# Mixture of layer 3 rebuilt around a slot map and adding scatters; self-attention in one straight run

## The chip, the cores and the metric

The kernel runs on one core of a Trainium2 chip. The metric is the device time of one launch in microseconds (us), the median over runs. In every run the whole program is executed: four layers, each of an attention and a feed-forward part.

## The reference, cut to what matters

The input `x` is 2 x 1024 tokens of 256 features in float32: 2048 tokens, 16 tiles of 128. Each layer adds `tanh(gate) * attention(layernorm(x))` and then `tanh(gate) * ffn(layernorm(x))` to `x`. The change touches layer 3 alone. Its attention part is a block of causal self-attention and cross-attention to 64 context rows, each with a small feed-forward part behind it:

```python
q = jnp.einsum('bsc,hcd->bhsd', xn, wq); k, v likewise        # 16 heads of 32
a = jax.nn.softmax(jnp.einsum('bhsd,bhtd->bhst', q, k) * D ** (-0.5), axis=-1)
if causal: a = a * mask                                        # the mask comes after the softmax
```

Since the mask comes behind the softmax, each row's maximum and sum are over all 1024 keys, and only the part below the diagonal is multiplied with the values. The feed-forward part of layer 3 is a mixture with the two best of eight experts for each token, plus a shared expert:

```python
probs = jax.nn.softmax(xn @ router_w, axis=-1)
topv, topi = jax.lax.top_k(probs, 2); topv = topv / jnp.sum(topv, axis=-1, keepdims=True)
for e in range(8): out = out + comb[:, e:e + 1] * swiglu(xn, gate_up_w[e], down_w[e])
out = out + swiglu(xn, shared_gate_up_w, shared_down_w)        # gate clipped to +-10, silu(gate) * up
```

An expert is 256 -> 2 x 1024 -> 256, the shared one 256 -> 2 x 256 -> 256.

## The kernel before, in words

The stages run one after the other; each is a block in which SP, POOL (gpsimd), PE (tensor), ACT (scalar) and DVE (vector) have instruction streams of their own, tied by semaphores. A stage's order is written out by hand. `ps` is PSUM with 8 banks, called `banks` in the profile.

**Cross-attention** (`stage_attention`, L336) folds the key weights into the queries (`fold_q`). Where `narrow` is false (L353; true for head width 16, so in layer 2) it folds the output weights into the values as well (`fold_v`, stored at L570): then 8 matmuls of 256 columns give a tile's output directly. Where it is true, values and output weights stay apart: 8 matmuls of 64 columns wide give the heads of a tile in a bank of their own, ACT stores them (`heads`, L708), 4 matmuls with the output weights follow, and the normalisation's transposes of the next tile (L222) wait in PE's order behind it. Layer 3 has head width 32, layer 0 has 64.

**Self-projection** (`stage_self_project`, L2028) computes queries, keys (in three bfloat16 parts each) and values, and writes them to DRAM by entry, an entry being 4 heads of one batch: `ENTRIES` = 8. SP issues eight DMAs for each pair of tiles k and, for batch 0 (k below 4), eight more into a ninth entry (`places`, L2064), so that the loop of the next stage can load one entry past the end. ACT's stores of the values (L2139) wait for the transfers out of their staging buffer. `load_entry` (L2015) loads an entry with 17 DMAs.

**Self-attention** (`stage_self_attention`, L2196) goes over 8 entries x 32 units (4 heads x 8 tiles of 128 queries). A unit v is: PE `scores` (L2292, 4 matmuls of 512 columns into two banks), DVE maximum (L2390), ACT exponential with row sum (L2373), DVE reciprocal (L2397), POOL multiplication by it (L2273) and mask (L2276), PE `turn` (L2308, 1 to 8 transposes of 128x128, up to four to a bankful), storing of them by ACT (L2359) or DVE (L2361), and `output` (L2326, four heads' matmuls for each chunk of 128 keys). The scores have two places, banks 0-1 and 2-3: `scores(v)` waits until the exponential of v-2 has read its place. Banks 4 and 5 take the turned tiles, banks 6 and 7 the outputs. PE's order for each v is scores(v), turn(v-5), a quarter of an output. ACT stores the outputs. Four entries make a body, and a hardware loop (`Fori`) runs it twice; at its turn the pipeline drains.

**The mixture** (`stage_experts`, L727, called for layer 3 as `l3f`) works in this order. PE computes router logits. DVE chooses the two best experts and, from counts by PE (`counted`, L961), works out for each token and choice a row number, a slot (DVE, L1159 to L1271). POOL scatters all rows of `xn` to those slots in DRAM by 32 indirect DMAs (L922) while PE runs the shared expert (L973, L984; eight pairs of tiles). Then come 24 expert tiles: 15 of 256 rows and 9 of 128 rows, 39 blocks of 128 rows in all (4992 rows for 4096 used). For each, SP loads the rows and the expert's weights, PE transposes (L999), computes hidden units (L1012, 64 matmuls) and output (L1025, 32 or 16), with DVE's clip (L1302), ACT's silu (L1077) and DVE's product between; ACT stores the result and POOL sends it to DRAM (L930). At the end POOL gathers 32 times (L939) the result rows of each token, DVE multiplies them by the routing weight and adds them to x (L1322), and SP sends x out by tile.

## Time and profile before

| what | value |
|---|---|
| median of 3 runs | 2548.7 us (2547.37 to 2549.26) |
| the profiled execution, its own time | 2524.31 us |
| span of its profile | 2522.6 us |
| mean granted TensorE clock | 0.902 |
| busy, share of the span | PE 81%, DVE 54%, ACT 37%, POOL 28% |
| DMA packets, data | 171504, 219.20 MB |
| chain that ended last | PE 17%, POOL 2%, issue 1%, DVE 1%, DMA 1% |

Time of the profiled execution is 2524.31 us, 1.7 us beyond its span. It lies 24.4 us (1.0%) under the median of the timed runs. The chain is the page's own: it starts in layer 3's mixture, so it says nothing of the stages before. A busy PE is one with matmuls in flight; the granted clock says at what speed, 0.9 being the mean in tenths of full speed.

### The profile page before, as it was taken

The numbers are of one execution on the slowest core, as the hardware profiler recorded it, in microseconds if no ns is written. First come the engines' busy times: TensorE is split into PE (matmuls) and PEld (weight loads), VectorE is DVE, ScalarE is ACT, GpSimd is POOL, SyncE is SP. The second block draws the span as 40 slices with busy tenths as digits, with TensorE's granted clock in tenths as the row PEclk, the third lists the DMA queues.
The fourth block names the chain that finished last, engine by engine and source line by source line (L and its number), as shares of the span: only waits on it lengthen the run. The fifth ranks groups of instructions, "written<-read, shape, count | busy, mean of one in ns | idle before, by whom it ended". The sixth has DMA issues, their size and how long they took to land. (4 is left out here: it accounts for less than half of the span.)

```text
span 2522.6 us, 36317 instructions
## 1 busy us (share of the span) xinstructions
PE 2047.2 (81%) x11904; PEld 1504.7 (60%) x11904; DVE 1367.6 (54%) x3511; ACT 929.6 (37%) x1859; POOL 710.5 (28%) x1199
## 2 busy tenths in 40 slices
PE   5983974467867677999799979969898589999991
PEld 4661863354444454555455558846687378888991
DVE  4871006535745765888688847757636432222332
ACT  4220321112324346888688843232232112222230
POOL 0223011030130125777577751102330230000005
PEclk9995995578979789999999989979999699999995
DMA  2004531000011286333333430110000525555684
GB/s 87 1 1 150 167 104 28 13 13 14 1 19 12 82 216 165 85 85 85 86 65 92 97 108 11 28 36 1 1 13 1 193 104 175 175 175 175 215 287 115
DMA packets 171504, 219.20 MB, mean 87 GB/s; under 512 B 39911, under 2 KB 133540, under 8 KB 165184
## 3 DMA queue, kind: packets, MB, share of 16 engines
q1 hardware_dynamic: 163344, 196.65, 26.7%
q0 software_dynamic: 7264, 20.31, 2.5%
q8 instruction: 88, 1.44, 0.2%
q14 instruction: 88, 0.72, 0.1%
q10 hardware_dynamic: 720, 0.07, 0.0%
HBM read 171.13 MB, written 46.14 MB: 86 GB/s over the span
## 5 line engine op out<-in xcount | busy, mean ns | idle before, releaser
L2390 DVE TENSOR_REDUCE l3s_mx<-banks 128x1 f32<-128x1024 f32 x256 | 313.1, 1223 | 96.7 <-PE banks L2292 93.8
L2292 PE MATMUL banks<-l_stack 128*128 128x512 bf16 x1024 | 268.1, 385 | 44.1 <-ACT xn_tokens L2373 21.0
L1012 PE MATMUL banks<-l3f_xrt,l3f_w 128*128 128x256 f32 (+1 forms) x1536 | 277.9, 342 | 2.7 <-issue 1.5
L1012 PEld LDWEIGHTS banks<-l3f_xrt,l3f_w 128*128 128x128 f32 x1536 | 249.6, 192 | 29.1 <-issue 3.3
L1302 DVE TENSOR_SCALAR l3f_sg<-banks 128x256 f32<-128x256 f32 (+1 forms) x192 | 72.0, 375 | 287.5 <-PE banks L1012 287.5
L2273 POOL TENSOR_TENSOR xn_tokens<-xn_tokens,l3s_sm 128x1024 f32<-128x1024 f32 (+3 forms) x128 | 201.6, 1575 | 50.3 <-DVE l3s_sm L2397 49.2
L222 PE MATMUL banks<-ident,xn_tokens 128*128 128x128 f32 x320 | 64.7, 338 | 166.8 <-DVE xn_tokens L211 148.0
L2292 PEld LDWEIGHTS banks<-l_stack 128*128 128x128 bf16 x1024 | 80.8, 98 | 163.3 <-ACT xn_tokens L2373 52.6
L2373 ACT ACTIVATE xn_tokens<-banks,l3s_mx 128x1024 f32<-128x1024 f32 x128 | 142.7, 1115 | 46.2 <-DVE l3s_mx L2390 45.1
L222 PEld LDWEIGHTS banks<-ident,xn_tokens 128*128 128x128 f32 x320 | 46.6, 172 | 188.4 <-DVE xn_tokens L211 133.0
L2373 ACT ACTIVATE x_features<-banks,l3s_mx 128x1024 f32<-128x1024 f32 x128 | 143.0, 1117 | 27.9 <-DVE l3s_mx L2390 27.6
L1077 ACT ACTIVATE l3f_sg<-l3f_sg 128x256 f32<-128x256 f32 (+1 forms) x192 | 72.2, 376 | 208.9 <-DVE l3f_sg L1302 208.9
L1025 PE MATMUL banks<-l3f_w,l3f_ht 128*128 128x256 f32 x624 | 138.5, 379 | 0.0
L930 POOL DMA_DIRECT2D l3f_results<-l3f_yt x24 | 15.8, 658 | 410.7 <-ACT l3f_yt L708 410.7
L1025 PEld LDWEIGHTS banks<-l3f_w,l3f_ht 128*128 128x128 f32 x624 | 116.8, 190 | 14.9
L2537 PE MATMUL banks<-x_features,weights 128*128 128x256 f32 x512 | 117.5, 390 | 4.3 <-ACT x_features L235 2.4
L2308 PEld LDWEIGHTS banks<-ident,xn_tokens 128*128 128x128 f32 x832 | 96.5, 140 | 29.1 <-issue 10.2
L2550 PE MATMUL banks<-weights,l3m_ht 128*128 128x256 f32 x512 | 113.2, 379 | 0.4 <-DVE l_x L2605 0.4
L2308 PE MATMUL banks<-ident,xn_tokens 128*128 128x128 f32 x832 | 112.6, 273 | 0.5 <-ACT l3s_pt L2359 0.5
L2537 PEld LDWEIGHTS banks<-x_features,weights 128*128 128x128 f32 x512 | 100.1, 196 | 19.5 <-issue 3.8
L2273 POOL TENSOR_TENSOR x_features<-x_features,l3s_sm 128x128 f32<-128x128 f32 (+3 forms) x128 | 92.4, 722 | 65.6 <-DVE l3s_sm L2397 64.6
L2359 ACT ACTIVATE l3s_pt<-banks 128x384 f32<-128x384 f32 (+2 forms) x192 | 97.0, 505 | 24.2 <-PE banks L2326 18.5
(532 smaller groups left out, 3925.4 us busy)
## 6 DMA issues: line engine op xcount, KB each, us to landing
l3f_w<-in_L_ffn_gate_up_w_dram SPq DMA_DIRECT2D x24, 2048.0 KB, 7.6
l3f_w<-in_L_ffn_down_w_dram SPq DMA_DIRECT2D x24, 1024.0 KB, 6.0
l_stack<-l_q_part SPq DMA_DIRECT2D x72, 256.0 KB, 6.0
l_stack<-l_k_part SPq DMA_DIRECT2D x72, 256.0 KB, 11.4
l0f_w<-in_L_ffn_W_dram SPq DMA_DIRECT2D x16, 1024.0 KB, 5.8
l_q_part<-l_stack SPq DMA_DIRECT2D x24, 256.0 KB, 3.0
l_k_part<-l_stack SPq DMA_DIRECT2D x24, 256.0 KB, 3.7
l3f_rows<-l3f_zero SPq DMA_DIRECT2D x13, 384.0 KB, 4.1
```

Source lines behind the costliest of these rows:

```text
L222: last = nc.tensor.transpose(ps[:, bank, c * PAIR + u * P:c * PAIR + (u + 1) * P], src(2 * j + u)[:, c * P:(c + 1) * P], core["ident"][:, :])
L1012: last = nc.tensor.matmul(ps[:, f % 4, h * PAIR:h * PAIR + size], w1_sb[:, p, dc, h * FF + f * P:h * FF + (f + 1) * P], xrt[:, p, dc, 0:si ...
L1025: last = nc.tensor.matmul(ps[:, 4 + p, u * D:(u + 1) * D], ht[:, p, f, u * P:(u + 1) * P], w2_sb[:, p, f, :], start=(f == 0), stop=(f == F ...
L1077: nc.scalar.activation(sg[:, f % 4, 0:size], sg[:, f % 4, 0:size], ACT.Silu).then_inc(silued, 1)
L2273: nc.gpsimd.tensor_tensor(ex[v % RING][:, si * P:], ex[v % RING][:, si * P:], sm[:, v % RING:v % RING + 1].to_broadcast([P, TOK - si * P]) ...
L2292: last = nc.tensor.matmul(ps[:, 2 * (v % 2) + h, :], stack[p][0][s][:, r, si * P:(si + 1) * P], stack[p][1][s][:, r, h * 512:(h + 1) * 512 ...
L2308: last = nc.tensor.transpose(ps[:, 4 + n % 2, c * P:(c + 1) * P], ex[v % RING][:, (si + c0 + c) * P:(si + c0 + c + 1) * P], core["ident"][ ...
L2359: last = op.activation(dst, src, ACT.Copy)
L2373: nc.scalar.activation(ex[v % RING][:, :], ps[:, 2 * (v % 2):2 * (v % 2) + 2, :].rearrange("p a n -> p (a n)"), ACT.Exp, bias=mx[:, v % RI ...
L2390: nc.vector.tensor_reduce(mx[:, v % RING:v % RING + 1], ps[:, 2 * (v % 2):2 * (v % 2) + 2, :].rearrange("p a n -> p (a n)"), AX_X, ALU.max ...
L2537: last = nc.tensor.matmul(ps[:, n % 4, 0:PAIR], w2[:, dc, f * P:(f + 1) * P], core["xt"][:, dc, PAIR * j:PAIR * (j + 1)], start=(dc == 0), ...
L2550: last = nc.tensor.matmul(ps[:, 4 + k % ring, u * D:(u + 1) * D], ht[:, k % 2, f, u * P:(u + 1) * P], w3[:, f, :], start=(f == 0), stop=(f ...
```

## The change

`stage_attention` takes the narrow form where the head width is at most 32 (before: at most 16). The self-projection writes no ninth entry. The self-attention is one straight run of 256 units with three places for scores (banks 0 to 5); turned tiles and outputs share banks 6 and 7 in alternation, an output's matmuls are done together, and the outputs are stored by ACT or DVE according to the bank; DVE stores ahead of its maximum. POOL multiplies in the form with a scalar operand.

A new function, `stage_top2`, takes the place of `stage_experts` in layer 3. It writes `xn` to DRAM by token and scatters no rows. From the slots DVE makes two tables, which of the 39 blocks a slot lies in (`spot`) and which of its 128 rows (`low_hot`); 32 matmuls turn them into a map from slot to token (`place`) and to routing weight (`share`). POOL gathers each block's rows by that map from the written `xn`, and after the expert adds them, already scaled by ACT (`store_y`), to the output in DRAM by an indirect DMA with an addition, each after the one before it has landed. The output holds x with the shared expert, written by SP before. The shared expert runs beside the routing: its clip, product and addition are POOL's, its PSUM copies, silu and scaling ACT's. The routing arithmetic up to the slots is the same. All 24 tiles are written out without a loop. Cut to what matters:

```diff
-    narrow = width * 4 <= KEYS
+    narrow = width * 2 <= KEYS
...
+def stage_top2(core, a, plan):
...
+                for h in range(2):
+                    at = slice(h * TILES // 2, (h + 1) * TILES // 2)
+                    sp.dma_start(xn_rows.rearrange("(t p) d -> p t d", p=P)[:, at, :], core["xn"][:, at, :]).then_inc(xn_sent, 16)
...
+                for q in range(PAIRS):
+                    sp.wait_ge(s_added, q + 1)
+                    sp.dma_start(a["out"].rearrange("b (t p) d -> p (b t) d", p=P)[:, 2 * q:2 * q + 2, :],
+                                 core["x"][:, 2 * q:2 * q + 2, :]).then_inc(begun, 16)
...
+                def shared_clip(n):
+                    pool.wait_ge(s_copied, n + 1)
+                    nc.gpsimd.tensor_scalar(su[:, n % 4, 0:PAIR], su[:, n % 4, 0:PAIR], 10.0, -10.0, ALU.min,
+                                            ALU.max).then_inc(s_clipped, 1)
+                def shared_multiply(n):
+                    q = n // SC
+                    pool.wait_ge(s_silued, n + 1)
+                    if q >= 2:
+                        pool.wait_ge(s_out_ready, q - 1)
+                    nc.gpsimd.tensor_tensor(s_ht[:, q % 2, n % SC, :], su[:, n % 4, 0:PAIR], su[:, n % 4, PAIR:2 * PAIR],
+                                            ALU.mult).then_inc(s_hid_stored, 1)
+                def shared_add(q):
+                    pool.wait_ge(s_out_stored, q + 1)
+                    x2 = pair_of(core["x"], q)
+                    nc.gpsimd.tensor_tensor(x2, x2, so[:, q % 2, :], ALU.add).then_inc(s_added, 1)
+                for n in range(SC * PAIRS + 1):
+                    if n < SC * PAIRS:
+                        shared_clip(n)
+                    if n >= 1:
+                        shared_multiply(n - 1)
+                    if n >= 2 * SC and n % SC == 0:
+                        shared_add(n // SC - 2)
+                shared_add(PAIRS - 1)
+                def gather(t):
+                    if t >= 2:
+                        pool.wait_ge(rows_turned, t - 1)
+                    for u in range(units(t)):
+                        at = blocks_through[t] + u
+                        pool.indirect_dma_start(xr[:, t % 2, u, :], None, xn_rows,
+                                                bass.IndirectOffsetOnAxis(ap=place[:, at:at + 1], axis=0),
+                                                bounds_check=T - 1, oob_is_err=False).then_inc(rows_in[t % 2], 16)
+                def scatter_add(t):
+                    pool.wait_ge(y_stored, t + 1)
+                    for u in range(units(t)):
+                        at = blocks_through[t] + u
+                        if at >= 1:
+                            pool.wait_ge(added, 16 * at)
+                        pool.indirect_dma_start(out_rows, bass.IndirectOffsetOnAxis(ap=place[:, at:at + 1], axis=0),
+                                                yt[:, t % 2, u, :], None, bounds_check=T - 1, oob_is_err=False,
+                                                compute_op=ALU.add).then_inc(added, 16)
+                pool.wait_ge(xn_sent, 32)
+                pool.wait_ge(places_made, 1)
+                gather(0)
+                gather(1)
+                pool.wait_ge(begun, 16 * PAIRS)
+                for t in range(tiles):
+                    if t + 2 < tiles:
+                        gather(t + 2)
+                    scatter_add(t)
+                pool.wait_ge(added, 16 * BLOCKS)
...
+                for j in range(PAIRS + 2):
+                    if j < PAIRS:
+                        for f in range(SC):
+                            shared_hidden(SC * j + f)
+                    if j == 2:
+                        pe.wait_ge(made, 9)
+                        pe.wait_ge(chosen, 1)
+                        nc.tensor.matmul(ps[:, 5, 0:P], tri[:, :], hots[:, :, :].rearrange("p t e -> p (t e)"),
+                                         start=True, stop=True)
+                        nc.tensor.matmul(ps[:, 6, 0:P], ones[:, :], hots[:, :, :].rearrange("p t e -> p (t e)"),
+                                         start=True, stop=True).then_inc(counted, 1)
+                    if j >= 2:
+                        shared_output(j - 2)
+                pe.wait_ge(spread, 1)
+                for n in range(2 * TILES):
+                    last = nc.tensor.matmul(ps[:, 7, 0:2 * BLOCKS], low_hot[:, n, :],
+                                            spot[:, n // TILES, n % TILES].rearrange("p a b -> p (a b)"),
+                                            start=(n == 0), stop=(n == 2 * TILES - 1))
+                last.then_inc(mapped, 1)
...
+                def shared_copy(n):
+                    act.wait_ge(s_hid_ready, n + 1)
+                    if n >= 4:
+                        act.wait_ge(s_hid_stored, n - 3)
+                    copy_bank(nc, su[:, n % 4, :], ps[:, n % 2, :]).then_inc(s_copied, 1)
+                def shared_silu(n):
+                    act.wait_ge(s_clipped, n + 1)
+                    nc.scalar.activation(su[:, n % 4, 0:PAIR], su[:, n % 4, 0:PAIR], ACT.Silu).then_inc(s_silued, 1)
+                def shared_store(q):
+                    act.wait_ge(s_out_ready, q + 1)
+                    if q >= 2:
+                        act.wait_ge(s_added, q - 1)
+                    nc.scalar.activation(so[:, q % 2, :], ps[:, 2 + q % 2, :], ACT.Copy, scale=gate).then_inc(s_out_stored, 1)
...
+                def store_y(t):
+                    p = t % 2
+                    act.wait_ge(out_ready, t + 1)
+                    if t >= 2:
+                        act.wait_ge(added, 16 * blocks_through[t - 1])
+                    for u in range(units(t)):
+                        at = blocks_through[t] + u
+                        last = nc.scalar.activation(yt[:, p, u, :], ps[:, 4 + p, u * D:(u + 1) * D], ACT.Copy, scale=share[:, at:at + 1])
+                    last.then_inc(y_stored, 1)
...
+                nc.vector.tensor_copy(flat(slot_i), flat(slot))
+                dve.drain()
+                ts(flat(slot_i), flat(slot_i), 7, None, ALU.arith_shift_right)
+                dve.drain()
+                nc.vector.tensor_copy(flat(slot_hi), flat(slot_i))
+                dve.drain()
+                stt(flat(slot), flat(slot_hi), float(-P), flat(slot), ALU.mult, ALU.add)
+                for k in range(2):
+                    tt(spot[:, k, :, 1, :], iota_hi[:, :].unsqueeze(1).to_broadcast([P, TILES, BLOCKS]),
+                       slot_hi[:, k, :].unsqueeze(2).to_broadcast([P, TILES, BLOCKS]), ALU.is_equal)
+                dve.drain()
+                for k in range(2):
+                    tt(spot[:, k, :, 0, :], spot[:, k, :, 1, :], token[:, :].unsqueeze(2).to_broadcast([P, TILES, BLOCKS]), ALU.mult)
+                dve.drain()
+                for k in range(2):
+                    tt(spot[:, k, :, 1, :], spot[:, k, :, 1, :], weight[:, k, :].unsqueeze(2).to_broadcast([P, TILES, BLOCKS]), ALU.mult)
+                dve.wait_ge(xn_sent, 32)
+                tt(low_hot, iota_lo[:, :].unsqueeze(1).to_broadcast([P, 2 * TILES, P]),
+                   flat(slot).unsqueeze(2).to_broadcast([P, 2 * TILES, P]), ALU.is_equal).then_inc(spread, 1)
+                dve.wait_ge(mapped, 1)
+                ts(place[:, :], ps[:, 7, 0:BLOCKS], float(NONE), None, ALU.add)
+                nc.vector.tensor_copy(share[:, :], ps[:, 7, BLOCKS:2 * BLOCKS]).then_inc(places_made, 1)
...
-                    if b == 0:
-                        places.append((ENTRIES, 1))
...
-    BODY = 4
...
+    SCORES = 3
...
-        with nc.Fori(0, ENTRIES // BODY) as jj:
...
+                    nc.gpsimd.tensor_scalar(ex[v % RING][:, si * P:], ex[v % RING][:, si * P:],
+                                            sm[:, v % RING:v % RING + 1], None, ALU.mult)
...
+                def output(w):
+                    e, si = w // KC, ORDER[w % KC]
+                    n = uses["out", w]
+                    for side in range(2):
+                        pe.wait_ge(stored[side], stored_through(side, max(last_turn[w], n - 2 if side == n % 2 else 0)))
+                    for c in range(si, KC):
+                        for r in range(R):
+                            last = nc.tensor.matmul(ps[r * W:(r + 1) * W, 6 + n % 2, 0:P],
+                                                    values[:, e % 2, c, r * W:(r + 1) * W],
+                                                    pt[:, w % 2, r, c - si, :], start=(c == si),
+                                                    stop=(c == KC - 1))
+                    last.then_inc(out_ready, 1)
...
+                for v in range(ENTRIES * UNITS + OUT):
+                    if v < ENTRIES * UNITS and v % UNITS == 0:
+                        e = v // UNITS
+                        pe.wait_ge(loaded[e % 2], 16 * LOADS * (e // 2 + 1))
+                    if v < ENTRIES * UNITS:
+                        scores(v)
+                    if v >= OUT and (v - OUT) % R == 0:
+                        output((v - OUT) // R)
+                    if TURN <= v < ENTRIES * UNITS + TURN:
+                        turn(v - TURN)
...
+            def _(dve):
+                for v in range(ENTRIES * UNITS + OUT + 1):
+                    store_output(dve, nc.vector, v - 1, 1)
+                    if v >= TURN + 1:
+                        store_turned(dve, nc.vector, v - TURN - 1, 1)
+                    if v < ENTRIES * UNITS:
+                        dve.wait_ge(scores_ready, v + 1)
+                        nc.vector.tensor_reduce(mx[:, v % RING:v % RING + 1],
+                                                ps[:, 2 * (v % SCORES):2 * (v % SCORES) + 2, :].rearrange("p a n -> p (a n)"),
+                                                AX_X, ALU.max, negate=True).then_inc(measured, 1)
+                    if 1 <= v <= ENTRIES * UNITS:
+                        dve.wait_ge(exped, v)
+                        nc.vector.reciprocal(sm[:, (v - 1) % RING:(v - 1) % RING + 1],
+                                             sm[:, (v - 1) % RING:(v - 1) % RING + 1]).then_inc(inverted, 1)
...
-    stage_experts(core, a, "l3f", top=2, full=TOP2_FULL, half=TOP2_HALF, capacity=None, plan=plans["l3f"], following=None,
-                  w1="L3_ffn_gate_up_w", w2="L3_ffn_down_w", swiglu=True, gate=core["gate_ffn"][:, 3:4],
-                  norm_behind=False)
+    stage_top2(core, a, plans["l3f"])
```

## Rows read from the trace of the kernel before

**Rows 1.** The chain that ended last, in order of time: start us, us, what

```profile
2050.68 16.38 PE banks L1012 x64
...
2462.37 6.92 PE banks L1025 x32
```

**Rows 2.** Timeline in self-attention: start us, us, engine, line, operation, out<-in, count [idle before]

```profile
1053.20 0.93 PE L2308 MATMUL banks<-ident,xn_tokens 128*128 128x128 f32 x7
...
1054.06 0.64 PE L2326 MATMUL banks<-l3s_pt,l_values_in 128*32 128x128 f32 x16
...
1054.64 1.04 PE L2292 MATMUL banks<-l_stack 128*128 128x512 bf16 x4
...
1055.57 0.95 PE L2308 MATMUL banks<-ident,xn_tokens 128*128 128x128 f32 x7
...
1056.46 0.42 PE L2326 MATMUL banks<-l3s_pt,l_values_in 128*32 128x128 f32 x8
...
1056.82 1.04 PE L2292 MATMUL banks<-l_stack 128*128 128x512 bf16 x4
...
1062.94 0.38 PE L2308 MATMUL banks<-ident,x_features 128*128 128x128 f32 x2
1063.14 1.22 DVE L2390 TENSOR_REDUCE l3s_mx<-banks 128x1 f32<-128x1024 f32 x1 [0.36 <-PE banks L2292]
...
1063.25 0.64 PE L2326 MATMUL banks<-l3s_pt,l_values_in 128*32 128x128 f32 x16
...
1065.77 0.61 PE L2292 MATMUL banks<-l_stack 128*128 128x512 bf16 x2
```

**Rows 3.** Groups at L2390 (ns min/median/max, first and last start), and the timeline mid-way

```profile
L2390 DVE TENSOR_REDUCE l3s_mx<-banks x256: 1201/1225/1227, 968.9 to 1468.6; 128x1 f32<-128x1024 f32 x128
...
1208.61 1.04 PE L2292 MATMUL banks<-l_stack 128*128 128x512 bf16 x4
...
1225.90 3.59 PE L2292 MATMUL banks<-l_stack 128*128 128x512 bf16 x8 [8.15 <-issue]
```

**Rows 4.** Waits from 825 to 970 us: engine, line <- releaser: us, times, longest

```profile
ACT l_stack L2139 <- DMA l_values<-l3p_vs: 10.5, 2, 9.0
```

**Rows 5.** Timeline of SP's queue: part of one loading of an entry

```profile
1050.60 3.88 SPq L2023 DMA_DIRECT2D l_stack<-l_k_part  x8
```

**Rows 6.** The cross-attentions: one group by form (L570), and timeline rows of PE

```profile
L570 ACT ACTIVATE l3a_fold_v<-banks x16: 384/384/385, 1669.7 to 1683.2; 128x256 f32<-128x256 f32 x16
...
1730.25 3.60 PE L499 MATMUL banks<-l3a_fold_q,x_features 128*128 128x512 f32 x8
1738.02 1.45 PE L499 MATMUL banks<-l3a_fold_q,x_features 128*128 128x512 f32 x3
...
650.22 1.11 PE L222 MATMUL banks<-ident,xn_tokens 128*128 128x128 f32 x4 [3.51 <-ACT l2a_heads L708]
```

**Rows 7.** Timeline of DVE in the routing of the mixture

```profile
1984.03 0.29 DVE L1159 COPY l3f_total<-banks 128x128 f32<-128x128 f32 x1 [0.50 <-PE banks L961]
...
2002.12 0.17 DVE L1271 COPY l3f_slot_f<-l3f_slot_f 128x16 f32<-128x16 f32 x1
```

**Rows 8.** Timeline of PE in the shared expert: two pairs of tiles

```profile
2031.56 3.62 PE L973 MATMUL banks<-x_features,weights 128*128 128x256 f32 x16
...
2036.74 0.59 PE L973 MATMUL banks<-x_features,weights 128*128 128x256 f32 x2
```

**Rows 9.** Timeline in the second feed-forward of layer 3: DVE beside POOL

```profile
1603.58 0.73 POOL L2507 TENSOR_TENSOR l_xo<-l_xo,weights 128x256 f32<-128x256 f32 x1
...
1603.71 0.61 DVE L150 SCALAR_TENSOR_TENSOR l3m_norm_rs<-l3m_norm_t,l3m_norm_rs 128x2 f32<-128x2 f32 x1
```

**Rows 10.** DMA issues of the page: engine, operation, count, KB each, us to landing

```profile
l3f_results<-l3f_yt POOLq DMA_DIRECT2D x15, 256.0 KB, 6.0
...
l3f_rows<-xn_tokens,l3f_slot POOLq DMA_INDIRECT x32, 2.5
```

**Rows 11.** The gathers of the end, grouped: ns min/median/max, first and last start

```profile
L939 POOL DMA_INDIRECT l3f_yg<-l3f_results,l3f_slot x32: 995/1002/1092, 2472.9 to 2513.4; - x32
```

More of the change, by code:

```diff
@@ L2089, in sent_before @@
             def sent_before(k):
-                return sum(16 * 8 * (2 if q < PAIRS // B else 1) for q in range(k % 2, k, 2))
+                return sum(16 * 8 for q in range(k % 2, k, 2))
             @block.gpsimd
@@ L2204, in stage_self_attention @@
     R, W = GROUP, L3_WIDTH
-    BODY = 4
     RING = 8
     TURN = 5
-    STORE = TURN
     OUT = TURN + R + 1
@@ new lines, in store_turned @@
+            def store_turned(eng, op, v, side):
+                if v >= ENTRIES * UNITS:
+                    return
+                e, w = v // UNITS, v // R
+                for g, (u, c0, size) in enumerate(groups):
+                    if u != v % UNITS or uses["turn", e, g] % 2 != side:
+                        continue
+                    n = BANKFULS * e + g
+                    eng.wait_ge(turned, n + 1)
+                    if w >= 2:
+                        eng.wait_ge(out_ready, w - 1)
+                    dst = pt[:, w % 2, v % R, c0:c0 + size, :].rearrange("p c n -> p (c n)")
+                    src = ps[:, 6 + side, 0:size * P]
+                    if side == 0:
+                        last = op.activation(dst, src, ACT.Copy)
+                    else:
+                        last = op.tensor_copy(dst, src)
+                    last.then_inc(stored[side], 1)
@@ new lines, in store_output @@
+            def store_output(eng, op, v, side):
+                if not OUT <= v < ENTRIES * UNITS + OUT or (v - OUT) % R != 0:
+                    return
+                w = (v - OUT) // R
+                e, si = w // KC, ORDER[w % KC]
+                if uses["out", w] % 2 != side:
+                    return
+                eng.wait_ge(out_ready, w + 1)
+                if e >= 2:
+                    eng.wait_ge(out_sent[e % 2], 16 * (e // 2))
+                dst, src = heads_out[:, e % 2, si * P:(si + 1) * P], ps[:, 6 + side, 0:P]
+                last = op.activation(dst, src, ACT.Copy) if side == 0 else op.tensor_copy(dst, src)
+                last.then_inc(stored[side], 1)
@@ L2404, in self_out_weights @@
+        clear_semaphores()
 def self_out_weights(a):
```

588 lines of the change are left out of this document (445 added, 143 removed).

## The prediction

> **What bounds the kernel now.** The page gives PE 81% busy, but its chain begins in the last mixture; so I read the chain for that stage and timelines for the others. In the mixture's main part the chain is PE without a gap [rows 1]: from 2050.68 us to 2462.37 + 6.92 = 2469.29 it takes 418.6 us for 39 blocks, 10.73 us each. What stands ahead (routing) and behind it (gathers) is latency, with PE short of work. In self-attention PE, DVE and ACT share a ring [rows 2, 3]; its 256 maxima span 499.7 us. Two things lie open there: the rate of a unit, and the turn of the loop. In the rest, the rows that the change touches are a wait for stored values [rows 4] and a cross-attention tile [rows 6].
>
> The profiled execution took 2524.3 us, 24.4 (1.0%) less than the median of 2548.7. I work out a difference against the former and subtract it from the latter. A measurement of this kernel can tell about 0.2%, 5 us.
>
> **Self-attention, rate.** By starts on PE [rows 2], seven transposes take 0.86 us (1053.20 to 1054.06), two 0.31: about 0.10 + 0.108 each. Two chunks of output (16 records) take 0.58, one 0.36: 0.14 for a piece and 0.22 for a chunk. Scores take 0.93. An entry has 32 units, 144 transposes, 36 chunks in 26 pieces: 29.8 + 18.8 + 11.6 = 60.1 us, 1.88 a unit. The ring of two score places is nearly as long: from a maximum (1063.14) to the scores that reuse the place (1065.77) 2.63, and 1.04 until they are done, with the hand-over 3.7 to 3.74 for two units, 1.87. Taking for each group of four units the larger of PE and 7.48 gives 60.9 us, 1.903 a unit. The maxima confirm it: 499.7 less the loop's turn (17.1, below) is 482.6 over 254 steps, 1.90.
> After the change an output is one piece: 8 pieces instead of 26 take 2.6 us off, 57.4 an entry, 1.79. Three places stretch the ring to 3.7/3 = 1.25, no bound. New is that turned tiles and outputs share two banks: an output's bank is stored by DVE or ACT before PE may go on with the second bankful. No row shows this; I add 0.04 a unit (a fifth of a 0.2 us wait), bounds 0 and 0.11, the latter eating all the gain. So 1.83, and (1.903 - 1.83) x 255 = 18.6 us.
> **The loop's turn.** Scores at 1208.61 are followed by the next at 1225.90 [rows 3]: 17.3 less one unit of 1.9 is 15.4, and the group behind it runs slower (eight records 3.59 where four take 1.04 [rows 2, 3]), 1.7 more. All 17 go. Together -35.6; bounds -46 (1.79 and 17) and -5 (a rate that gets 0.05 worse).
>
> **Self-projection.** ACT waits 10.5 us in two waits [rows 4] for values to be sent, the longest behind SP's loading of the first entry. SP spends 3.88 us on eight issues [rows 5], 0.49 each; the eight ninth-entry writes of pair 3 stand ahead, 3.9 us of queue and 0.5 MB. -4, bounds 0 (the transfers end last whatever SP does) and -8.
>
> **Cross-attention of layer 3, narrow.** Sixteen stores less, of 0.384 us plus hand-over, 0.43 [rows 6]: -6.9. The values must be built twice over instead: two products of 512 columns and two DVE copies, +2.7. A tile took 7.77 us (1730.25 to 1738.02); a pair of tiles now 16.0. The new one has fewer columns, 14.5, but PE waits behind the stored heads as layer 2's does (3.51 us for ACT) [rows 6], of which a half is filled by the next scores: 16.2. With a longer tail (1.5) +2 net; bounds -6 and +12 (the wait in full at several tiles, then slower scores behind it).
>
> **Mixture, head.** Now: DVE has the counts at 1984.03 and the slots at 2002.12 [rows 7], 82 small instructions in 18.1 us, then POOL scatters and hidden starts at 2050.68 [rows 1]. After: the hidden groups of three pairs stand ahead of the counts, 3 x 3.62 [rows 8] = 10.9, half of it beside DVE's choice of experts: counts at 1989.6. From there DVE runs beside POOL, which has per pair two clips (up to 0.73 each), two products of 0.73 and an addition of up to 1.46 [rows 9]: about 3.7 us of each 5.18 [rows 8]. One row shows what that does: a DVE instruction with two inputs took 0.61 where small ones take 0.17, started 0.13 behind POOL's 0.73 [rows 7, 9]. Of the 82, 49 are of such a kind (two inputs or a scalar operand). So DVE completes about 10.9 of them a pair, and the slots come at 2025, not 2007.6. Behind them: split and tables, 6 operations of 624 elements and one of 4096, 10.6 -> 2035.6; the map's 32 products, as 32 of 128 columns 6.9 (16 of 256 columns take 6.92 [rows 1]), at half that speed 13.8, I take 9.5 -> 2045; places 0.6; two gathers, 1.3 and 2.5 [rows 10, 11] -> 2050; transposes and their store 2.0 -> 2052.1. The 32 scatters of 1.3 and the load behind them are gone, yet the head ends 1.5 us later. SP's two writes of xn and its eight of x (issue 0.49 each) lie beside this; if cover fails, the eight delay only POOL's first addition into the output, not PE.
> The Trainium skill (SBUF — State Buffer, Who interferes with whom) has the shared port pair as an exclusive lock, and counts DVE's copies and casts among what takes it, which no row here shows; by that 75 of the 82 are blocked and the head gives +5.5 instead of +1.5. It has a chance of its own below.
>
> **Mixture, main part.** The same tiles and PE work: 0. What covers the new parts: POOL has per full tile two gathers (1.3 each) and two additions into DRAM, each issued when the last has landed; a plain store lands in 6.0 beside the weights, a lone scatter in 2.5 [rows 10]. At 1.3 + 2.5 to 1.3 + 6.0 a block takes 3.8 to 7.3, with its gather 5.1 to 8.6, under 10.73.
> The Trainium skill (Collectives: The Full Stack, The bandwidth ceiling: the fold count and why AG ≠ RS ≠ AR) says that an addition in the DMA path needs two source reads and gets about half the throughput. No row here shows it; doubling the landing would lead to the slower rival below.
>
> **Mixture, tail.** Now from 2469.3 to the span's end 2522.6, 53.3 us, most of it 32 gathers at 1.31 (2472.9 to 2513.4) [rows 11]. After: store 0.6, the previous addition's rest 2, issue 1.0, landing 3 (bounds 2.5 and 12), closing 2.8: 9. -44.3, bounds -47 and -30.
>
> **Sum.** -35.6 - 4 + 2 + 1.5 + 0 - 44.3 = -80.4: the profiled execution at 2443.9, the median at 2468.3.
>
> **Rivals.**
> A. *The lock does not bite*: the row of 0.61 is chance, or POOL's new work finds gaps. The slots come at 2007.6; then the shared expert, PE-bound, ends about 2026 and the chain gives hidden at 2037.5, -13 instead of +1.5. Sum -95, 2454. For it: most small DVE operations in the trace last 0.17; against: POOL is hardly ever busy beside them now. 0.15.
> B. *Copies and casts are locked out too*: +5.5, sum -76, 2472. 0.07.
> C. *Shared banks take the place of the score ring*: PE waits for each output's store, the unit stays at 1.903; only the loop's turn is gained. -80.4 + 18.6 = -62, 2487. For it: DVE stores an output a unit late, and its 1.22 us maximum stands in front [rows 2]. 0.15.
> D. *Slower: the additions become a serial chain.* They are strictly one after the other, 39 of them. If one takes L, 39 L binds once L is above 10.73, and the kernel is slower than before from 39 L = 414.8 + 80, L = 12.7. Rows give 3.8 to 7.3; with a landing of twice 6.0 it is 1.3 + 12 = 13.3, and POOL's gathers queue behind the wait. At L = 14: +131 - 80 = +51, 2600. 0.06.
> E. *Nothing is gained*, because the straight program's instruction stream or an unseen wait gives it all back: within 5 us of 2548.7. 0.02.
>
> **How the numbers follow.** The forecast has 0.55; its own range, from the bounds of the terms (self-attention and tail mostly), is 2448 to 2490. A, B and C lie at 2454, 2472 and 2487, so a range of 2432 to 2500 holds them with their own spread and leaves out D and E and both far ends. Faster by over 0.2%: 0.55 + 0.15 + 0.07 + 0.15 = 0.92; within: 0.02; slower: 0.06.
>
> **What would show it.** In self-attention: maxima spanning about 467 us, no gap mid-way, PE's waits at L2292 for ACT gone; waits for stored bankfuls would show C. In the head: DVE's small operations at 0.3 to 0.6 beside POOL, the map's products near 2036 to 2045 (times relative to the stage's begin), hidden 87 us behind that begin; at 72 it is A. In the main part 10.7 a block; idle PE behind late gathers would show D, read from the additions' issue to landing. The tail about 9 us. I am wrong if the main part grows, or if self-attention stays near 1.90 a unit.

## The result, and the profile after

The changed kernel takes 2557.3 us (median of 7 runs, 2550.6 to 2561.3) against 2546.3 for the kernel before, in the same runs: ratio 1.0043, 95% interval 1.0028 to 1.0058. It is slower by 0.4%, where the forecast was faster by 3.2%; the measured time lies 57 us above the upper end of the range, 2500. The profiled execution took 2550.6 us with a span of 2549.1.

I cut both profiles at the same marks: begin of the self-projection (tiles `l3p`), first maximum and last maximum of self-attention (DVE's group of L2390, now L2953), SP's first load of the next stage (tiles `l3m`), begin of the cross-attention (tiles `l3a`), first store of router logits, DVE's first copy of the counts, first hidden product and last output product of the mixture. Differences of those starts, in us:

| stretch | before | after | forecast of the difference | measured |
|---|---|---|---|---|
| begin to self-projection | 818.5 | 815.6 | 0 | -2.9 |
| self-projection to first maximum | 150.5 | 147.8 | -4 | -2.7 |
| first to last maximum | 499.7 | 540.0 | -35.6 | +40.3 |
| last maximum to the next stage | 12.8 | 18.0 | 0 | +5.2 |
| self-attention's feed-forward | 179.4 | 178.2 | 0 | -1.2 |
| cross-attention and its feed-forward | 308.4 | 301.7 | +2 | -6.7 |
| logits to hidden (routing) | 81.4 | 82.2 | +1.5 | +0.8 |
| first hidden to last output product | 418.6 | 453.9 | 0 | +35.3 |
| to the span's end | 53.4 | 11.6 | -44.3 | -41.8 |

Two rows carry the miss: self-attention (with the 5.2 us behind its last maximum) and the mixture's main part. The costliest groups of the page of after; behind the bar: busy us, mean ns | idle before, releaser:

```profile
L2953 DVE TENSOR_REDUCE l3s_mx<-banks 128x1 f32<-128x1024 f32 x256 | 311.2, 1218 | 75.8 <-PE banks L2852 75.0
L2837 POOL TENSOR_SCALAR xn_tokens<-xn_tokens,l3s_sm 128x1024 f32<-128x1024 f32 (+3 forms) x128 | 303.0, 2367 | 15.2 <-DVE l3s_sm L2958 15.2
...
L2837 POOL TENSOR_SCALAR x_features<-x_features,l3s_sm 128x128 f32<-128x128 f32 (+3 forms) x128 | 139.1, 1086 | 0.1
```

POOL's two groups are busy 442 us of self-attention's 540, and with the 256 masks of 0.29, 75 us, it has next to no idle time: it waited 15 us for the first unit and then for nobody.

In the mixture's main part I read the distance from one tile's transposes to the next. Where [rows 1] had PE without a gap, the chain of after goes through DMAs. At the change from full tiles (256 rows) to half tiles (128 rows):

```profile
2405.31 5.40 DMA out_dram<-l3f_yt,l3f_place
...
2413.35 6.75 DMA l3f_xr<-l3f_xn,l3f_place
...
2420.83 8.81 PE banks L1614 x32
```

POOL still issues the two additions of a full tile, the second when the first has landed, and a gather behind them, while PE has only a half tile's hidden units (7.31 us instead of 13.98) to fill the time. PE idled 9.3 us there, and 9.3 once more a tile later. A little later, one half tile around, the timeline shows the round trip with one addition (start us, us, engine, line):

```profile
2463.64 0.47 ACT L1686 ACTIVATE l3f_yt<-banks,l3f_share 128x256 f32<-128x256 f32 x1 [2.34 <-PE banks L1614]
...
2464.89 1.58 POOL L1509 DMA_INDIRECT out_dram<-l3f_yt,l3f_place  x1 [7.85 <-ACT l3f_yt L1686]
...
2466.78 1.07 POOL L1499 DMA_INDIRECT l3f_xr<-l3f_xn,l3f_place  x1 [0.31 <-issue]
...
2471.98 0.44 PE L1588 MATMUL banks<-ident,l3f_xr 128*128 128x128 f32 x2 [1.23 <-DMA l3f_xr<-l3f_xn,l3f_place]
...
2475.91 0.47 ACT L1686 ACTIVATE l3f_yt<-banks,l3f_share 128x256 f32<-128x256 f32 x1 [2.65 <-PE banks L1614]
```

A result is stored, POOL issues its addition (1.58), then the gather of the rows that PE transposes next (in the program it is three tiles on from the one just stored); the rows land 5.2 us later, PE transposes them, and only behind those transposes stands the next output. From store to store: 12.27 us, where the kernel without this wait (e3 below) takes 10.82.

### The profile page after: what moved, and what is told of

It reads as the page before. It is cut to its first block and busy times, and to the rows that moved or that the text cites. A ratio compares the mean times of both kernels' runs of the same rounds, so it can differ in the third digit from the quotient of the medians.

```text
span 2549.1 us, 35782 instructions
## 1 busy us (share of the span) xinstructions
PE 2031.5 (80%) x12060; PEld 1506.6 (59%) x12060; DVE 1362.3 (53%) x3476; ACT 946.5 (37%) x1865; POOL 909.5 (36%) x1235
## 5 line engine op out<-in xcount | busy, mean ns | idle before, releaser
L2953 DVE TENSOR_REDUCE l3s_mx<-banks 128x1 f32<-128x1024 f32 x256 | 311.2, 1218 | 75.8 <-PE banks L2852 75.0
L2837 POOL TENSOR_SCALAR xn_tokens<-xn_tokens,l3s_sm 128x1024 f32<-128x1024 f32 (+3 forms) x128 | 303.0, 2367 | 15.2 <-DVE l3s_sm L2958 15.2
L222 PE MATMUL banks<-ident,xn_tokens 128*128 128x128 f32 x320 | 64.3, 336 | 173.4 <-DVE xn_tokens L211 147.8
L1509 POOL DMA_INDIRECT out_dram<-l3f_yt,l3f_place x39 | 62.1, 1593 | 347.7 <-ACT l3f_yt L1686 275.5
L2868 PE MATMUL banks<-ident,xn_tokens 128*128 128x128 f32 x832 | 126.1, 282 | 68.7 <-POOL xn_tokens L2840 60.6
L2868 PEld LDWEIGHTS banks<-ident,xn_tokens 128*128 128x128 f32 x832 | 89.3, 140 | 124.9 <-POOL xn_tokens L2840 100.4
L222 PEld LDWEIGHTS banks<-ident,xn_tokens 128*128 128x128 f32 x320 | 45.7, 171 | 196.5 <-DVE xn_tokens L211 126.0
L2912 ACT ACTIVATE l3s_pt<-banks 128x384 f32<-128x384 f32 (+3 forms) x224 | 109.4, 489 | 115.8 <-PE banks L2868 115.2
L2852 PEld LDWEIGHTS banks<-l_stack 128*128 128x128 bf16 x1024 | 101.0, 99 | 82.2 <-issue 16.2
L2837 POOL TENSOR_SCALAR x_features<-x_features,l3s_sm 128x128 f32<-128x128 f32 (+3 forms) x128 | 139.1, 1086 | 0.1
L1614 PEld LDWEIGHTS banks<-l3f_w,l3f_ht 128*128 128x128 f32 x624 | 120.2, 196 | 16.3
L2914 DVE COPY l3s_pt<-banks 128x384 f32<-128x384 f32 (+3 forms) x160 | 88.1, 551 | 56.6 <-PE banks L2868 55.5
```

What stands on the lines that cost most here:

```text
L222: last = nc.tensor.transpose(ps[:, bank, c * PAIR + u * P:c * PAIR + (u + 1) * P], src(2 * j + u)[:, c * P:(c + 1) * P], core["ident"][:, :])
L1614: last = nc.tensor.matmul(ps[:, 4 + p, u * D:(u + 1) * D], ht[:, p, f, u * P:(u + 1) * P], w2_sb[:, p, f, :], start=(f == 0), stop=(f == F ...
L2837: nc.gpsimd.tensor_scalar(ex[v % RING][:, si * P:], ex[v % RING][:, si * P:], sm[:, v % RING:v % RING + 1], None, ALU.mult)
L2852: last = nc.tensor.matmul(ps[:, 2 * (v % SCORES) + h, :], stack[p][0][s][:, r, si * P:(si + 1) * P], stack[p][1][s][:, r, h * 512:(h + 1) ...
L2868: last = nc.tensor.transpose(ps[:, 6 + n % 2, c * P:(c + 1) * P], ex[v % RING][:, (si + c0 + c) * P:(si + c0 + c + 1) * P], core["ident"][ ...
L2912: last = op.activation(dst, src, ACT.Copy)
```

## The experiments

My theory after this reading: two independent losses, POOL's scalar form in self-attention and the gather that stands behind the addition.

### e1_gather_ahead, e2_pool_two_inputs, e3_both

e1:

```diff
                 gather(1)
+                gather(2)
                 pool.wait_ge(begun, 16 * PAIRS)
                 for t in range(tiles):
-                    if t + 2 < tiles:
-                        gather(t + 2)
+                    if t + 3 < tiles:
+                        gather(t + 3)
                     scatter_add(t)
```

e2:

```diff
-nc.gpsimd.tensor_scalar(ex[v % RING][:, si * P:], ex[v % RING][:, si * P:],
-                        sm[:, v % RING:v % RING + 1], None, ALU.mult)
+nc.gpsimd.tensor_tensor(ex[v % RING][:, si * P:], ex[v % RING][:, si * P:],
+                        sm[:, v % RING:v % RING + 1].to_broadcast([P, TOK - si * P]), ALU.mult)
```

e3 has both. Expected:

> The changed kernel, with each tile's gathers issued one step earlier, ahead of the addition that they stood behind. Theory 1 (a loop: output, store, addition, gather of the tile after next, its transposes, which stand ahead of the next output on PE): the loop is cut, full tiles go from 21.5 to 21.2 us, half tiles from 12.2 to 10.8, the main part from 450 to about 420, the kernel from 2557 to about 2527. Rival (the additions themselves are the chain, 39 of them one after the other, or they slow the gathers' transfers): the main part stays at 440 or more, the kernel above 2545.

> The changed kernel, with POOL's multiplication in self-attention in the form of before (two inputs, the second spread along the row) instead of the scalar operand. Theory 1 (POOL bounds self-attention since the scalar form takes 2.37 us where the other took 1.58): the 256 maxima span about 468 us instead of 540, the kernel comes to about 2485. Rival (the shared banks, or the new order, hold PE back, and POOL is only busy): the span stays above 520, the kernel above 2535. If between, both: about 490 us would be the old rate of 1.90.

> Both edits together. Theory 1: the two losses are independent and add up: about 2557 - 30 - 72 = 2455, faster than before by 3.6%; the prediction's sum was 2468. Rivals: each as above; above 2500 if either holds.

Measured: e1 2518.7 us, ratio to the kernel before 0.9893 (0.9874 to 0.9912); e2 2483.2, 0.975 (0.9731 to 0.9769); e3 2450.0, 0.9621 (0.9603 to 0.9639). In e1 the main part is 418.1 us instead of 453.9, in e2 the maxima span 476.9 instead of 540.0; each leaves the other stretch as it was to within 3 us, and together they take 107 us off. Both rivals fall: neither a chain of additions nor the shared banks made the kernel slow. What the earlier issue did is seen in the waits of PE's weight loads (PEld) for the gathers in the main part, first of after, then of e3 (us, times, longest):

```profile
PEld banks L1588 <- DMA l3f_xr<-l3f_xn,l3f_place: 33.2, 19, 9.5
```

```profile
PEld banks L1589 <- DMA l3f_xr<-l3f_xn,l3f_place: 0.2, 1, 0.2
```

### e4_before_scalar_form

The kernel before with e2's edit the other way round. Expected:

> The kernel before, with only POOL's multiplication in the scalar form. Theory 1: POOL needs 2.02 us and gaps, some 2.1 us a unit, above the 1.90 that the score ring gave: the maxima span about 540 + 15 us for the loop's turn, the kernel 2546 + 50 = 2596. Rival (the form costs only in the new order): within 10 us of 2546.

Measured: 2608.5 us, ratio 1.0242 (1.0223 to 1.0261); the maxima span 556.5 us, 56.8 more. The form costs much the same in either order: 57 us of span and 63 of the median here; in the new order 63 us of span and 69 to 74 of the median (e1 against e3, after against e2). Some 5 us of it lie behind the last maximum (there 21.6 us to the next stage's first product where e13, the kernel before again, has 16.3). The groups of POOL by form in e4 and in the kernel before (ns min/median/max, the largest form has 1024 elements):

```profile
L2273 POOL TENSOR_SCALAR xn_tokens<-xn_tokens,l3s_sm x128: 1884/2365/2858, 970.4 to 1524.2; 128x1024 f32<-128x1024 f32 x32, 128x896 f32<-128x896 f32 x32, 128x768 f32<-128x768 f32 x32, 128x640 f32<-128x640 f32 x32
```

```profile
L2273 POOL TENSOR_TENSOR xn_tokens<-xn_tokens,l3s_sm x128: 1254/1576/1897, 971.8 to 1465.0; 128x1024 f32<-128x1024 f32 x32, 128x896 f32<-128x896 f32 x32, 128x768 f32<-128x768 f32 x32, 128x640 f32<-128x640 f32 x32
```

1024 elements take 2.86 us in the form with a scalar from memory and 1.90 with two inputs: (2.858 - 1.884) / 384 = 2.5 ns an element against 1.7.

### e5_two_places

`SCORES = 2` in e3. Expected:

> e3_both with two places for scores instead of three; turned tiles and outputs still share banks 6 and 7. In e3_both the 256 maxima span 477 us, 1.87 a unit, where the prediction had 1.83 and PE's own work 1.79. Theory (the third place earns the gain, the shared banks cost some of it): with two places the ring's 1.87 and the shared banks' waits come together, 1.92 to 2.0 a unit, a span of 490 to 510, the kernel 13 to 33 us above e3_both. Rival (the third place does nothing, all of the gain is the loop's turn): the span stays within 4 us of 477.

Measured: 2500.2 us; the maxima span 526.3, 2.06 a unit, more than expected. So in the new order the third place earns 0.19 a unit, not 0.03 (1.90 before, 1.87 in e3): with two places the new order is slower than the old one. The reason is argued, not shown by a run of its own: DVE's stores now stand ahead of its maximum and ACT's stores of outputs ahead of its exponential, and these stores lengthen the ring of scores. Waits of PE's weight loads from 1000 to 1400 us in e5, then in e3 (us, times, longest):

```profile
PEld banks L2853 <- ACT xn_tokens L2943: 50.5, 72, 1.2
```

```profile
PEld banks L2881 <- ACT l3s_pt L2913: 31.1, 27, 1.6
```

In e5 the scores (L2853) wait for the exponential; in e3 that wait is gone from the list and the output (L2881) waits longer for the stores of turned tiles instead (15.3 us in e5).

### e6_plain_scatter

The addition of e3 left out (`compute_op` gone). Expected:

> e3_both with the indirect DMA of the results into the output as a plain write instead of an addition (what lies there already is overwritten, so the other expert's share and x are left out). Theory (an addition costs the DMA path a second read, but nobody waits for it since the gathers are ahead): POOL's wait for the landing of a tile's first one falls from 4.6 us to 2 to 4, the main part stays at 418, the kernel within 5 us of e3_both. Rival (the addition is no dearer than a write): the wait stays at 4.6.

Measured: 2448.3 us, main part 417.8. POOL's waits for a landing, counted from the end of its issue, are 71.4 us in 15 waits, in e3 68.9 in 15. The rival holds for the landing: beside the weights' loading an addition lands no later than a write. The issue itself is dearer, 1.58 us against 1.02, so from one issue to the next that waits for it 6.2 us pass instead of 5.7 (medians). The Trainium skill's rule that an addition needs two source reads and so gets half the throughput (Collectives: The Full Stack, The bandwidth ceiling: the fold count and why AG ≠ RS ≠ AR; stated there for large collectives) does not show at this size, 128 KB by rows of 1 KB.

### e7_pool_two_columns

```diff
-nc.gpsimd.tensor_scalar(su[:, n % 4, 0:PAIR], su[:, n % 4, 0:PAIR], 10.0, -10.0, ALU.min,
+nc.gpsimd.tensor_scalar(su[:, n % 4, 0:2], su[:, n % 4, 0:2], 10.0, -10.0, ALU.min,
```

and likewise for product and addition, so that most of POOL's work on the shared expert is left out; ACT's silu writes `s_ht`. Expected:

> e3_both with POOL's clip, product and addition of the shared expert on 2 columns only (the product and most of the clip and of the addition are left out; ACT's silu writes what PE reads). Theory (POOL locks DVE out while routing is worked out): from the counts to the slots 18 to 19 us instead of 30, to the first hidden unit 46 to 52 instead of 65, of which part is that the map's products follow PE's work without a gap and so run at the higher clock (7 us instead of 14); the kernel 13 to 19 us below e3_both. Rival (DVE is slow for another cause, such as PE's traffic): 28 us or more to the slots, the kernel within 4 us of e3_both.

Measured: 2435.1 us; 48.4 from counts to hidden instead of 64.9. DVE in after, with a POOL row of the same time:

```profile
2018.62 0.29 DVE L1746 COPY l3f_total<-banks 128x128 f32<-128x128 f32 x1 [2.73 <-PE banks L1570]
...
2021.11 1.27 POOL L1483 TENSOR_TENSOR x_tokens<-x_tokens,l3f_so 128x512 f32<-128x512 f32 x1 [2.77 <-ACT l3f_so L1652]
2021.21 1.20 DVE L1779 COPY l3f_rows_f<-l3f_scan 128x8 f32<-128x8 f32 x1
...
2050.36 1.16 DVE L1848 CAST l3f_slot_hi<-l3f_slot_i 128x32 f32<-128x32 int32 x1
```

A copy of 8 elements takes 1.20 us while POOL adds for 1.27. The same cast in e7, and the map's products in after and in e7:

```profile
1969.66 0.18 DVE L1851 CAST l3f_slot_hi<-l3f_slot_i 128x32 f32<-128x32 int32 x1
...
1984.38 7.27 PE L1578 MATMUL banks<-l3f_spot,xn_tokens 128*128 128x78 f32 x64
```

```profile
2061.74 13.94 PE L1577 MATMUL banks<-l3f_spot,xn_tokens 128*128 128x78 f32 x64 [9.44 <-DVE xn_tokens L1861]
```

The cast takes 0.18 instead of 1.16: DVE was held back by POOL, copies and casts included. And the products take half the time when they follow PE's other work.

### e8_wide_l3a and e12_ninth_entry

Two parts of the change undone in e3: `narrow = width * 4 <= KEYS`, and the writes of the ninth entry. Expected:

> e3_both with layer 3's cross-attention in its form of before. From its begin to the router's logits of the mixture e3_both takes 302.1 us and the kernel before 308.4. Theory (the narrow form itself saves 6 us, where the prediction had a loss of 2): back to 308, the kernel 6 us above e3_both. Rival (the difference comes from another place, such as what the stage before leaves): within 2 us.

> e3_both with the ninth entry's writes restored. From the self-projection's begin to the first maximum: 147.1 us in e3_both, 150.5 in the kernel before. Theory (the writes stand ahead of SP's loading): back to 150.5, the kernel 3 us above e3_both; within the noise of the median, but seen in the profile. Rival (the 3 us come from the loop's setup): 147 stays.

Measured: e8 2459.7 us, 311.2 from the cross-attention's begin to the logits instead of 302.1: the narrow form saves 9, a little more than expected. e12 took 149.5 us from the self-projection's begin to the first maximum instead of 147.1, so the writes cost 2.4. Its median, 2458.5, is 8.5 above e3's, of which this explains a third; stretches that the edit does not touch were longer as well (821.8 instead of 816.2 up to the self-projection). I take the stretch, and leave the rest open.

### e10_filler_twice

```diff
+                for n in range(20):
+                    nc.tensor.matmul(ps[:, 4, 0:PAIR], s1[:, 0, 0:P], core["xt"][:, 0, 0:PAIR], start=True, stop=True)
                 pe.wait_ge(spread, 1)
```

and 12 more ahead of the first tile's transposes. Expected:

> e3_both with matmuls whose result nobody reads, 20 ahead of the map's products and 12 ahead of the first tile's transposes, so that PE is not idle before them. In e3_both PE idles 9.4 us, then the map's 32 products take 13.95 us at a granted clock of 0.50; where they followed work without a gap (POOL on 2 columns) they took 7.27. Theory (the idle time costs the clock): the map takes 7 us, the first tile's hidden products 14 instead of 15.6, from counts to hidden 57 to 58 instead of 64.9, the kernel 7 to 10 us below e3_both. Rival (the products are slow in themselves, through their weights, and the fillers only delay): the same or up to 8 us slower.

Measured: 2441.2 us, ratio 0.9591 (0.9578 to 0.9604), 57.8 us from counts to hidden. The windows of after around the map and of e10 (us, PE, PEld, DVE, ACT and POOL busy, granted clock, DMA share, GB/s):

```profile
2048.00:2062.00 14.00, 2.26 (x9) 1.70 (x10) 12.81 (x13) 1.68 (x3) 4.58 (x6) 0.78 1.02 397
2062.00:2076.00 14.00, 13.68 (x64) 13.46 (x64) 0.28 (x2) 0.00 (x0) 0.00 (x0) 0.50 0.53 181
```

```profile
1995.00:2003.00 8.00, 7.79 (x67) 7.74 (x68) 0.46 (x3) 0.00 (x0) 0.00 (x0) 1.00 0.99 338
```

In after PE was busy 2.3 of 14 us, and the products behind ran at a granted clock of 0.50, the 1.2 GHz level, and took 13.94 us. With matmuls nobody reads in that gap the same products ran at 1.00, 2.4 GHz, and took 7.37 us. The rival falls.

### e11_output_later and e14_all_together

e11 is e3 with `OUT = TURN + R + 2`; e14 has e10's and e11's edits. Expected:

> e3_both with each output of self-attention one unit later (OUT one more). In e3_both PE waits at the output for ACT's and DVE's stores of turned tiles, some 50 us over 400. Theory (the output stands too close behind the last store in the shared banks): the waits halve and the maxima span 465 to 473 us instead of 477. Rival (what is waited for is the store of the use just before in the same bank, which moves along): the same within 3 us, or slower.

> e3_both with both later edits, the matmuls that keep PE busy in the head and the outputs one unit later. Theory (they work in different stages and add up): the maxima span 469 us, 57.8 from counts to hidden, the kernel 2449 - 8 - 7 = 2434. Rival (one's gain is given back, as layer 3's cross-attention took 2.6 us longer in the profile of e11): 2440 or more.

Measured: e11 2442.9 us, the maxima span 468.6, 1.84 a unit. The weight loads' waits at the output for ACT's stores fall from 31.1 to 12.3 us between 1000 and 1400; new ones for POOL's masks appear, 23.7 us. e14: 2434.1 us, ratio 0.9553 (0.9539 to 0.9567), maxima 468.8, counts to hidden 57.7: the gains add up. e14 is the fastest of the complete kernels here, 4.5% below the kernel before.

### e13_before_again and e15_four_scatters

The profile that the prediction used lay 22 us under its kernel's median. e13 is the kernel before, unchanged; e15 leaves 28 of the mixture's 32 scatters out. Expected:

> The kernel before, unchanged, profiled again. Its profile gave 2524.3 us, 22 below its median of 2546; the other kernels' profiles lie 2 to 7 below theirs. The kernel before with the scalar form showed, while POOL issued its 32 scatters, two stretches of 9.0 and 14.3 us in which DVE stood still beside the shared expert, and 91.8 us from counts to hidden instead of 66.6. Theory (DVE stands still behind POOL's scatters in most executions, once or twice, and the profiled one was a lucky one): this profile is near 2541 to 2546, with 80 to 92 us from counts to hidden. Rival (the profile is low in general and the stretch belongs to the scalar form): about 2524 again, 66.6 us.

> The kernel before with 4 of the mixture's 32 scatters of rows (the others are left out; their rows stay zero, and the expert tiles do the same work on them). The kernel before, profiled again, had DVE's clip of the shared expert standing still for 8.4 and 15.0 us while POOL issued the scatters, and 91.9 us from counts to hidden. Theory (POOL's issuing of indirect transfers holds DVE's instruction back): no such wait; PE's shared expert then sets the head, 18 us to the slots, some 42 us of shared expert, 2 behind it: 62 to 66 us from counts to hidden, the kernel 25 to 30 us below the one before, at about 2518. Rival (the stand-still comes with something else, such as the loading of weights or of code at that time): 80 us or more, within 10 us of 2546.

Measured: e13 2548.5 us, its profiled span 2545.5 with 91.9 us from counts to hidden, where the first profile had 66.6. All other stretches agree within 2 us. In e13:

```profile
2031.07 0.42 DVE L1276 TENSOR_SCALAR l3f_sg<-banks 128x256 f32<-128x256 f32 x1 [8.42 <-remote]
...
2046.45 0.42 DVE L1276 TENSOR_SCALAR l3f_sg<-banks 128x256 f32<-128x256 f32 x1 [14.96 <-remote]
...
2047.25 3.23 PE L973 MATMUL banks<-x_features,weights 128*128 128x256 f32 x7 [26.83 <-DVE l3f_ht L1284]
```

DVE stands still twice, 23.4 us together, and PE waits with it. The first stand-still lies within POOL's issues of its scatters, one every 1.28 us (2001.5 to 2042.2); the second begins there and ends 4.2 us behind the last one. e15: 2513.3 us, ratio 0.9867 (0.9848 to 0.9886), 62.5 us from counts to hidden and no such wait: 35 us under the kernel before where 25 to 30 were expected, 29 of them in this stretch against e13. So it comes with the scatters. The first profile caught an execution without it; its 2524.3 us lie below every timed run of the kernel before (2538 to 2553), and the two later profiles of this head (e4, e13) both have it. e15 takes the issues, the transfers and whatever queues behind them away together: which of these holds DVE back (the loading of code, named in the rival, is not excluded), and why it did not in that one execution, no run here shows.

## Why the prediction was wrong

**Self-attention, POOL.** The sum had no term for "POOL multiplication becomes the scalar form", though the diff shows it; it was silently costed at nothing. It makes POOL the bound: 540.0 / 255 = 2.12 us a unit. The cover was thin: before, POOL had 294.0 us of multiplication and 75 of masks in 499.7; with the new form the same work is 442 + 75 = 517 us, more than the stretch had. This is the largest error, 540.0 - 476.9 = 63 us, and the 5.2 behind the last maximum go with it.

**Self-attention, rate and loop's turn.** With the form of before the span is 477, and I had 467 (1.83 against 1.87). The turn of the loop was right: 17 of the 23 us saved are the gap of [rows 3], the rest is the rate. The term that was mis-sized is the shared banks' 0.04: if PE's own 1.79 is right, 0.08 is left for it. Moving the output by a unit gets 0.03 back. Rival C had the right banks and not the right wait: it had PE wait for the store of an output (7.4 us of the weight loads' waits in e3's 400), and PE waits ahead of the output for stores of turned tiles (31.1 for ACT's). "Three places stretch the ring to 1.25" was too favourable, since the ring became longer in the new order: with two places it runs at 2.06, not 1.87.

**Mixture, main part.** The step that failed is "a block takes 3.8 to 7.3, with its gather 5.1 to 8.6, under 10.73". Its numbers were right: an addition takes 1.6 + 4.6 = 6.2 us. But I compared POOL's throughput with PE's, and the order makes a round trip of latencies: output, store, addition, gather, landing (5.2, not the 2.5 of [rows 10]), transposes, next output. 3.47 + 0.47 + 0.8 + 1.9 + 5.2 + 0.4 gives 12.2 for a half tile; measured 12.27 where PE needs 10.82. In a full tile there is a second addition and gather, and it takes 21.4 to 21.6 instead of 21.16. These steady tiles are the smaller part: against e3 the full tiles lose 6 us (2.5 of them in one tile, where a landing was late) and the last half tiles 6. The other 24 of the 36 us are lost in the three tiles at the change of size, where a full tile's two additions and a landing of 6.7 us stand against a half tile's work: two waits of 9.3, and outputs behind them that take 9.00 and 6.22 us instead of 7.07 and 3.62, at granted clocks of 0.75 and 0.58. An average of 10.73 a block hides that place. Rival D saw gathers behind the wait, but priced it by the additions' chain, which alone never bound.

**Mixture, head.** Forecast +1.5, measured +0.8 against the same profile: luck, with errors that cancel. Counts came 2.4 us later, not 5.6; 30.2 us from there to the slots, not 35.4; the tables 12.9, not 10.6; the map 13.95, not 9.5, because PE idled before it. Rival B was right about the kinds: the copy of 1.20 and the cast of 1.16 above agree with the lock of the Trainium skill (SBUF — State Buffer, Who interferes with whom), which counts copies and casts in; e7 shows the whole price of POOL's work beside DVE, 16.5 us, of which 6.7 are the map's clock. Its sum of +5.5 was still further off than +1.5, since the other errors cancel. Rival A falls.

**Mixture, tail.** -41.8 for -44.3: after the last output product 11.6 us remain, not 9 (the terms of the 9 add up to 9.4). The last addition is issued at 2538.85, 1.4 us behind it, and 10.2 us before the span's end, where I had 1 + 3 + 2.8.

**Cross-attention.** -6.7 for +2. The loop was right: 16.46 us for a pair of tiles (1767.90 to 1784.36), forecast 16.2. The recorded terms do not add up to +2: -6.9 + 2.7 + 1.5 and eight pairs at 16.2 instead of 16.0 give -1.1. Three stretches make the -6.7. From the begin to the first query product it is 17.2 us instead of 22.8: the setup gains most of the folds, and the price of building the values twice (+2.7) hardly shows. The query products span 111.2 instead of 114.1, since the second and third pair, before the loop is steady, take 4.1 less. From the last of them to the logits it is 1.8 more, for the +1.5 of the tail.

**Self-projection.** -2.7 for -4; e12 puts 2.4 on the writes.

**The base.** Working from one profiled execution hid an effect of the change itself: the 32 scatters cost 25 us by holding DVE back (91.9 against 66.6) in both later profiles and, by the medians, in most executions, not in that one. The change takes the scatters out and so gains these 25 us, which no term of the sum holds; without this gain the changed kernel would be, by my estimate, 11 + 25 = 36 us slower than before. So the forecast for a kernel without the two faults was too high: 2468 where e3 took 2450. Against e13's span, after gives 2549.1 - 2545.5 = +3.6; against the first profile, which the sum of -80.4 was made for, +26.5, while the medians differ by 11.

## What to carry to other kernels

Price every changed form of an instruction, also on an engine with idle time: one word in POOL's multiplication cost 63 us and more. Where an engine gets a wait in its queue, follow what stands behind it round to the same engine: a sum of latencies in one order is a bound of its own, and issuing a load one step earlier removed it. Look for it where the sizes change: most of the loss lay in three of 24 tiles. And when a profile lies further under its median than its fellows do, profile the same kernel once more before trusting it.

## What the runs showed of the hardware

- POOL's multiplication with a scalar from memory takes 2.5 ns an element, with two inputs, the second spread along the row, 1.7 (f32, 128 partitions); yet its clip with two constants took 0.40 us for 256 elements where a product of two inputs took 0.73.
- DVE stood still for 8.4 and 15.0 us during and just behind 32 indirect transfers issued by POOL in a row (e13; 9.0 and 14.3 in e4), and ran freely with four (e15) and in one profile with all 32.
- A DVE copy of 8 elements took 1.20 us beside POOL's addition of 1.27, and a cast of 32 took 1.16, 0.18 without POOL's work.
- An indirect DMA with an addition took 1.58 us to issue where the same without one took 1.02 (a gather 1.07), and after the issue it landed no later than the plain write (4.6 against 4.8 us of waiting, means of 15).
- The granted clock was 0.50 for the 14 us behind a stretch in which PE was busy for 2.3 of 14 us, and 1.00 when that stretch was filled.
